# Audio-tower kernel on Trainium2: overflow rows of the tree feed-forward in groups of 128 with one leaf, tiles in pairs, levels added by halving

## What is computed

```
for _ in range(DEPTH + 1):                      # 8 levels
    all_nodes.append(current)
    score = jnp.einsum('td,td->t', flat_x, w1s[current]) + b1s[current]
    all_logits.append(score)
    choice = ((jnp.sign(score) + 1.0) / 2.0).astype(jnp.int32)
    current = current * 2 + choice + 1
path_weights = jax.nn.gelu(jnp.abs(logits), approximate=False)
for i in range(DEPTH + 1):
    t_i = jnp.einsum('td,tdo->to', flat_x, w2s[nodes_i]) + b2s[nodes_i]
    out = out + t_i * path_weights[:, i][:, None]
```

## Time and profile before

| what | value |
|---|---|
| device time, median of 3 runs | 558.85 us (558.7 to 559.1) |
| span of the profiled execution | 558.3 us |
| PE busy | 378.6 us (68%) |
| DVE busy | 369.1 us (66%) |
| ACT busy | 290.4 us (52%) |
| POOL busy | 273.7 us (49%) |
| DMA | 36.05 MB, mean 65 GB/s |

### The profile page before, as it was taken

One profiled execution on the slowest core, in us unless ns is written; L12 is line 12 of the kernel. 1 busy time (PEld: TensorE's weight loads), 2 busy tenths in 40 slices (PEclk: granted clock), 3 DMA queues, 4 the chain that ended last, 5 costly groups with the idle time before them and its releaser, 6 DMA issues.

```text
span 558.3 us, 8700 instructions
## 1 busy us (share of the span) xinstructions
PE 378.6 (68%) x3014; PEld 251.9 (45%) x3014; DVE 369.1 (66%) x596; ACT 290.4 (52%) x652; POOL 273.7 (49%) x316
## 2 busy tenths in 40 slices
PE   1212487888889978899588895475107997487781
PEld 1212353444547645476355652364105775254450
DVE  1295148777887779877878679625774999542431
ACT  1103466999986999869698695101101110144441
POOL 3036385333322468633658613838555777742211
PEclk9999997999999999999989998555557999599996
DMA  3500269839323332223303400380004110200000
GB/s 81 110 1 0 53 150 214 191 71 211 80 53 84 84 82 56 47 67 84 83 4 92 103 1 1 71 142 0 19 13 125 36 44 24 73 9 5 7 5 8
DMA packets 54530, 36.05 MB, mean 65 GB/s; under 512 B 25122, under 2 KB 53687, under 8 KB 54480
## 3 DMA queue, kind: packets, MB, share of 16 engines
q1 hardware_dynamic: 51538, 32.97, 27.7%
q0 software_dynamic: 2944, 2.45, 1.6%
HBM read 10.57 MB, written 8.79 MB: 35 GB/s over the span
## 4 chain that ended last, share of the span: by engine, by line
ACT 29%; PE 27%; DVE 25%; issue 8%; DMA 3%; SPq 3%; POOL 2%; POOLq 0%; DVEq 0%; ACTq 0%
ACT S L884 16%; PE S L697 6%; DVE nm L1031 5%; PE U L643 5%; DVE lm L1203 4%; ACT vT L871 4%; ACT k L871 3%; ACT q L871 3%; DVE vT L1196 3%; PE S L797 3%; PE U L604 2%; DMA vT<-in_L_attn_Wqkv 2%; PE U L797 2%; PE S L799 1%; SPq L282 1%
## 5 line engine op out<-in xcount | busy, mean ns | idle before, releaser
L1031 DVE TENSOR_REDUCE nm<-S 128x1 f32<-128x748 f32 x192 | 171.9, 932 | 44.3 <-PE S L697 41.7
L884 ACT ACTIVATE S<-S,nm 128x748 f32<-128x748 f32 x192 | 166.8, 883 | 42.4 <-DVE nm L1031 41.1
L697 PE MATMUL S<-pool_a 128*128 128x512 f16 (+1 forms) x768 | 151.4, 333 | 28.6 <-ACT S L884 26.0
L697 PEld LDWEIGHTS S<-pool_a 128*128 128x128 f16 x768 | 69.0, 105 | 91.4 <-ACT S L884 57.6
L520 POOL DMA_INDIRECT out<-lm,vT x44 | 43.3, 985 | 58.2 <-DVE lm L1209 51.2
L442 POOL TENSOR_TENSOR pool_a<-q,pool_a 128x750 f16<-128x750 f32 x16 | 25.8, 1610 | 82.4 <-DVE pool_a L1025 82.4
L604 PE MATMUL U<-xhT,wq 128*128 128x250 f16 x288 | 43.4, 292 | 21.0 <-ACT k L871 10.1
L1203 DVE TENSOR_REDUCE lm<-vT 128x64 f32<-128x512 f32 x44 | 45.1, 1026 | 1.3
L604 PEld LDWEIGHTS U<-xhT,wq 128*128 128x128 f16 x288 | 26.9, 104 | 39.6 <-ACT k L871 15.9
L884 ACT ACTIVATION_READ_ACCUMULATOR S<-S,nm 128x1 f32 x192 | 43.5, 226 | 0.0
L1196 DVE TENSOR_TENSOR vT<-vT 128x512 f32<-128x512 f32 x12 | 8.3, 693 | 41.9 <-ACT vT L953 41.9
(11 more groups left out here) (214 smaller groups left out, 666.8 us busy)
## 6 DMA issues: line engine op xcount, KB each, us to landing
pool_a<-pool_a SPq DMA_DIRECT2D x64, 187.5 KB, 3.0
pool_a<-pool_a SPq DMA_DIRECT2D x64, 93.8 KB, 2.8
sorted_rows<-zrow SPq DMA_DIRECT2D x1, 3864.0 KB, 22.6
vT<-sorted_rows SPq DMA_DIRECT2D x11, 276.0 KB, 3.7
w<-in_L_ffn_w2s SPq DMA_DIRECT2D x1, 2048.0 KB
lm<-in_x SPq DMA_DIRECT2D x4, 375.0 KB
pool_a<-in_L_ffn_w2s SPq DMA_DIRECT2D x1, 1024.0 KB
vT<-in_L_attn_Wqkv SPq DMA_DIRECT2D x2, 384.0 KB, 9.3
```

The source lines that it names most:

```text
L697: last = mm(S[n % 3][:, c0:c1], kst[:, u % 3, a, hd, START[t]:START[t] + P], qst[:, u % 3, hd, c0:c1], start=(a == 0), stop=(a == 1))
L884: sc_.activation(S[n % 3][:, 0:N], S[n % 3][:, 0:N], ACT.Exp, bias=nm[:, b % 2, j, i:i + 1], accum_out=sm[:, b % 2, j, i:i + 1]).then_inc( ...
L1031: v.tensor_reduce(nm[:, b % 2, j, i:i + 1], S[n % 3][:, 0:N], X, ALU.max, negate=True).then_inc(s_max, 1)
```

## The change

- **Groups.** An overflow group has 128 rows of one leaf and is a tile of its own. There is still space for 96 groups, which are now 96 tiles; `sorted_rows` grows from 7168 to 16384 rows, and SP fills it in four parts (w = 1 to 4), `w7` moves to w == 5. With the inputs given there are 29 groups, and 15 pairs of tiles run.
- **Products.** Levels 0 to 5 stand together in one table of 32 entries with six matrices each, so one product of 384 columns takes the place of those of 256 and 128; level 6 has a table `w6`. An overflow tile needs three products over all 128 rows; results lie where DVE wants them, so ACT's copies and `yv` go. Only the 65 rows in use are contracted, so POOL's zeros go.
- **Pairs.** Everything from `load_rows` to `add_residual` works on two tiles. A block `If` holds one pair instead of four tiles: 48 blocks, of which 15 run and 33 are skipped.
- **Sums.** The strided reduction becomes three halving additions (`levels_4`, `levels_2`, `levels_1`).
- **Order.** PE and ACT prepare pair m + 1 ahead of pair m, also across the border of the stages; SP loads the first overflow pair ahead of reading `nact`.
- **Space.** `xhT`, `wq`, `q32` and `k32` move into `pool_a`, which `wlow` and `w6` take over later.

```diff
...
-SLOTS = STAT + OVG * G
-ST_TILES, OV_TILES = STAT // P, OVG * G // P
+SLOTS = STAT + OVG * P
+ST_TILES, OV_TILES = STAT // P, OVG
 F_TILES = ST_TILES + OV_TILES
+FILLS = 4
...
-                if w == 1:
+                if 1 <= w <= FILLS:
 
                     sp.wait_ge(s_id, 2)
-                    sp.dma_start(rows.rearrange("(t p) c -> p t c", p=P),
-                                 zrow[:].unsqueeze(1).to_broadcast([P, F_TILES, RW])).then_inc(s_fill, 16)
...
+                    fl = slice((w - 1) * F_TILES // FILLS, w * F_TILES // FILLS)
+                    sp.dma_start(rows.rearrange("(t p) c -> p t c", p=P)[:, fl, :],
+                                 zrow[:].unsqueeze(1).to_broadcast([P, F_TILES // FILLS, RW])).then_inc(s_fill, 16)
+                if w == FILLS + 1:
...
             sp.wait_ge(s_score, 2 * NT * NU)
...
+            sp.wait_ge(s_prod, NU)
+            tv = wlow[:, 0:n_low].rearrange("p (n l o) -> p n l o", n=NODES5, l=6)
+            for rows_, src in ((slice(0, D), wv), (slice(D, D + 1), b2s.unsqueeze(0))):
+                for lv in range(6):
+                    n = 2 ** lv
+                    r = NODES5 // n
+                    m = D if src is wv else 1
+                    if n <= r:
+                        for i in range(n):
+                            sp.dma_start(tv[rows_, i * r:(i + 1) * r, lv, :],
+                                         src[:, n - 1 + i:n + i, :].to_broadcast([m, r, D])).then_inc(s_low, 16)
+                    else:
+                        for q in range(r):
+                            sp.dma_start(tv[rows_, q::r, lv, :], src[:, n - 1:2 * n - 1, :]).then_inc(s_low, 16)
+                sp.dma_start(w6[rows_, 0:2 * NODES5 * D].rearrange("p (n o) -> p n o", o=D),
+                             src[:, 2 * NODES5 - 1:4 * NODES5 - 1, :]).then_inc(s_low, 16)
...
+            def load_rows(m):
+                if m >= NX:
+
+                    for k in range(2 * (m - NX), 2 * (m - NX) + 2):
+                        sp.wait_ge(s_outr[k % NO], 16 * (k // NO + 1))
+                sp.dma_start(xs[:, m % NX], rv[:, 2 * m:2 * m + 2, :]).then_inc(s_xsr[m % NX], 16)
+
+            for m in range(ST_PAIRS):
+                load_rows(m)
             sp.wait_ge(s_goff, 1)
             sp.wait_ge(s_sego, 16 * TT)
+            load_rows(ST_PAIRS)
             groups = sp.value_load(nact[0:1, 0:1], min_val=0, max_val=OVG)
-            for k in range(ST_TILES // 4, F_TILES // 4):
-                with sp.If(groups > 4 * (4 * k - ST_TILES)):
-                    load_rows(k)
+            for m in range(ST_PAIRS, F_PAIRS - 1):
+                with sp.If(groups > 2 * (m - ST_PAIRS)):
+                    load_rows(m + 1)
...
-                       start=True, stop=True)
-                    mm(y[:, 7 * D:8 * D], xg, w7all[:, bass.ds(node(g, 0) * D, D)],
-                       start=True, stop=True).then_inc(s_y, 1)
-                return following
-
-            pe.wait_ge(s_goff, 1)
+            def overflow_pair(m):
+                leaves = [nc.tensor.value_load(lami[0:1, 2 * (m - ST_PAIRS) + t:2 * (m - ST_PAIRS) + t + 1],
+                                               min_val=0, max_val=LEAVES - 1) for t in range(2)]
+                pair_ready(m)
+                for t in range(2):
+                    y = y_banks(m)[:, 512 * t:512 * (t + 1)]
+                    xk = xsT[:, m % 3, t * P:(t + 1) * P]
...
+            for m in range(ST_PAIRS):
+                if m == 2:
+                    pe.wait_ge(s_goff, 1)
+                xs_T(m + 1)
+                static_pair(m)
             groups = pe.value_load(nact[0:1, 0:1], min_val=0, max_val=OVG)
-            for m in range(ST_TILES // 4, F_TILES // 4):
-                with pe.If(groups > 4 * (4 * m - ST_TILES)):
-                    xs_T(m)
-                    pairs = load_leaves(4 * m)
-                    for k in range(4 * m, 4 * m + 4):
-                        pairs = overflow_products(k, pairs)
+            for m in range(ST_PAIRS, F_PAIRS):
+                with pe.If(groups > 2 * (m - ST_PAIRS)):
+                    if m + 1 < F_PAIRS:
+                        xs_T(m + 1)
+                    overflow_pair(m)
...
-                    act.wait_ge(s_y, banks(4 * (m - 2)))
...
+                    act.wait_ge(s_y, m - 2)
+                sc_.copy(xsT[:, m % 3, :], S[0][0:D + 1, 512 * (m % 2):512 * (m % 2) + 2 * P]).then_inc(s_xc, 1)
+
+            for m in range(ST_PAIRS + 1):
                 path_weights(m)
                 xs_copy(m)
...
-            for m in range(ST_TILES // 4, F_TILES // 4):
-                with act.If(groups > 4 * (4 * m - ST_TILES)):
-                    path_weights(m)
-                    xs_copy(m)
-
-                    for k in range(4 * m, 4 * m + 4):
-                        if k >= ST_TILES + 2:
-                            act.wait_ge(s_wy, k - 1)
-                        for g in range(4):
-                            act.wait_ge(s_y, banks(k) + g + 1)
-                            sc_.copy(yv[g * G:(g + 1) * G, k % 2, :],
-                                     y_bank(banks(k) + g)[0:G, :]).then_inc(s_yv, 1)
+            for m in range(ST_PAIRS, F_PAIRS - 1):
+                with act.If(groups > 2 * (m - ST_PAIRS)):
+                    path_weights(m + 1)
+                    xs_copy(m + 1)
...
-            def weigh(k):
...
+            def weigh(m):
...
+                wk = xs[:, m % NX, :, C_W:C_H]
+                v.tensor_tensor(wy[:, m % 2], y_banks(m)[:].rearrange("p (t l o) -> p t l o", t=2, l=DEPTH),
+                                wk.unsqueeze(3).to_broadcast([P, 2, DEPTH, D]), ALU.mult).then_inc(s_wy, 1)
+
+            def levels_4(m):
+                dve.wait_ge(s_wy, m + 1)
+                w = wy[:, m % 2]
+                v.tensor_tensor(w[:, :, 0:4, :], w[:, :, 0:4, :], w[:, :, 4:8, :], ALU.add).then_inc(s_s1, 1)
+
+            def levels_2(m):
+                dve.wait_ge(s_s1, m + 1)
+                w = wy[:, m % 2]
+                v.tensor_tensor(w[:, :, 0:2, :], w[:, :, 0:2, :], w[:, :, 2:4, :], ALU.add).then_inc(s_s2, 1)
+
+            def yo_pair(m):
+                return yo[:, 2 * m % NO:2 * m % NO + 2, :]
+
+            def levels_1(m):
+                for k in range(2 * m, 2 * m + 2):
+                    if k >= NO:
+                        dve.wait_ge(s_outr[k % NO], 16 * (k // NO))
+                dve.wait_ge(s_s2, m + 1)
+                w = wy[:, m % 2]
+                v.tensor_tensor(yo_pair(m), w[:, :, 0, :], w[:, :, 1, :], ALU.add).then_inc(s_sl, 1)
+
+            def add_residual(m):
+                dve.wait_ge(s_sl, m + 1)
+                o = yo_pair(m)
+                v.tensor_tensor(o, o, xs[:, m % NX, :, C_H:C_ID], ALU.add).then_inc(s_yo, 1)
+
+            for m in range(ST_PAIRS):
+                weigh(m)
+                if m >= 1:
+                    levels_1(m - 1)
+                levels_4(m)
+                if m >= 1:
+                    add_residual(m - 1)
+                levels_2(m)
+            levels_1(ST_PAIRS - 1)
+            add_residual(ST_PAIRS - 1)
             dve.wait_ge(s_goff, 1)
             groups = dve.value_load(nact[0:1, 0:1], min_val=0, max_val=OVG)
-            for m in range(ST_TILES // 4, F_TILES // 4):
-                with dve.If(groups > 4 * (4 * m - ST_TILES)):
-                    for k in range(4 * m, 4 * m + 4):
-                        weigh(k)
-                        sum_levels(k)
-                        add_residual(k)
+            for m in range(ST_PAIRS, F_PAIRS):
+                with dve.If(groups > 2 * (m - ST_PAIRS)):
+                    weigh(m)
+                    levels_4(m)
+                    levels_2(m)
+                    levels_1(m)
+                    add_residual(m)
...
```

229 lines of the change are left out of this document (72 added, 157 removed).

## The result

The changed kernel takes **587.56 us** (median of four runs, 587.39 to 588.28), the kernel before 558.98 beside it (558.7 to 559.36): a ratio of 1.0511, 95% interval 1.0496 to 1.0526. The forecast was 556.5 us, its range 549 to 566. It was wrong by 31 us and in the sign. The profiled execution took 587.61 us, its span is 585.9.

The account below looks back on a forecast made before the run. DVE and POOL nearly fill the static stage; overflow is a chain of waits. Overflow's 58.5 us become 49.2; of 9.3 won, 3.7 go to later start, 1.3 to the second output, 2 to the end: 556.5 us, range 549 to 566.

Parts of the forecast that it names:

- The first pair: Start of the static stage: DVE needs two tiles before weighing, so the first output comes 4.3 us later, at 434.3.
- The static stage: Static tiles cost nothing more: DVE 2.94 us a pair, PE about 3.1, both hidden behind POOL's 5.1.
- The overflow stage: Overflow tiles: DVE bounds at 3.28 us a pair, PE 3.0 to 3.5; 15 pairs take 49.2 us, last residual at 543.0.
- list of what costs nothing: Fill, table loads, POOL's zeros and DVE's packing, mostly ahead of the static stage: costed at nothing; 1 to 3 us if units wait.
- Nothing before 415 us changes in a way that I can cost at more than its cover: Everything ahead of the static stage: no change there counted, so the sum covers only about the last 143 us.
- The border: Static to overflow: PE idles some 12 us for overflow rows, restarts at the lower clock; first overflow weighing at 493.8.
- The end: After the last output at 545.1: 33 skipped blocks on every engine, SP, POOL and PE ending near 555, span 556.
- rival 2: End of the kernel: POOL's closing drain is a fixed 8 us behind its skips, giving 559.9 us; chance 0.18.
- rival 1: End of the kernel: PE's way through the skipped blocks takes 28.2 us and ends last, giving 563.5 us; chance 0.14.
- Rival 3: Overflow tiles: PE bounds at 3.6 us a pair if register loads stop it and its clock falls, 561 us; chance 0.12.
- The fill: Filling sorted_rows ahead of the static stage: grows from 3.9 to 9 MB, costed at nothing, 1 to 3 us if units wait.

Follow-up runs that it names:

- fourth set: Changed kernel with 128 rows contracted in the 384-column products only, their table's zeros written by ScalarE, empty overflow pairs skipped eight at once: 553.32 us, 0.9898 of the kernel before.
- the blocks: POOL and SP skip empty overflow pairs eight at once, against the changed kernel with 128 rows and its zeros moved (582.90 us): 579.19 us, 0.9855 of the kernel before.

## Why the prediction was wrong

The step that failed is in "The first pair" and "The static stage": the clock of the earlier trace rows, 0.93, was carried over to products whose operands had changed from 128 rows to 65. The same holds for PE's price in "The overflow stage", 1024 columns at 1.8 ns: 3.0 to 3.5 us a pair by it, 4.58 measured at 0.50, so that PE bounds the pair and not DVE. In the forecast's list of what costs nothing, the zeros appear only as "POOL's zeros end 33 us before they could matter". That the rows they fill take part in every product, and what a product of fewer rows does to the clock, was not asked. Point by point:

- **The first pair**: first output 4.3 us later, at 434.3. Measured 430.28. From the transposes to it, it is 14.2 us against 7.7, so 6.5 later by itself, 2.2 more than forecast. The forecast had the upper level from the second tile on, as before, where it came 4.2 us behind the first transpose. That was wrong apart from the 65 rows: with 128 rows on the fourth set's chip it came 9.5 us behind it, and the first output after 13.6 us. But the stage starts at 416.1, 6.3 us earlier. "Nothing before 415 us changes in a way that I can cost at more than its cover" was wrong.
- **The static stage** costs nothing more: right in its result, wrong in its reason. POOL went on without a gap up to 477.16 (forecast 479.3), in 46.9 us for the 45.0 forecast, as some scatters took up to 1.5 us and not 0.98; PE at 5.05 us a pair instead of 3.1 is just as fast as POOL's 5.1 to 5.2, by chance.
- **The border**: 12 us idle, restart at the lower clock, first overflow weighing at 493.8. In the changed kernel PE never idles there, it is late itself, and that weighing is at 502.7. With 128 rows (fourth set) PE idles 12.46 us and the weighing comes at 492.3.
- **The overflow**: DVE 3.28 us a pair, PE 3.0 to 3.5. Measured: PE 4.58, DVE waiting 1.4 us in each pair. Fourteen pitches of 1.30 us more make 18.2 us (67.4 us from the first weighing to the last residual at 570.1, 49.2 forecast), the largest term of the miss. With the clock up, DVE took 3.07 and PE less (it waited for DVE's banks); the stage took 46.3 us against 49.2 forecast.
- **The end**: SP 9.8 us behind the last output, measured 9.3; POOL's skips 5.6 us, measured 5.4, of which 1.0 lie ahead of the last output's start; its closing step lasts 9.06 us from its own start, behind the skips (8.0 before), and does not end 8.6 us after the last output. That is rival 2, and it came: 13.7 us of tail, not 10. PE's walk past the empty blocks took 15.9 us (561.3 to 577.2), 20 forecast, 28.2 under rival 1, which fell: 5 waits of 0.6 to 2.0 us in it, none of 3.9.
- **Rival 3** (PE bounds the overflow if "its clock falls again") had the right engine and the wrong cause and size: 3.6 us a pair for a fall after idling, where PE never idled and needed 4.58.
- **The fill** (1 to 3 us lost at most): it lost nothing, and its four pieces are half of what won 5.5 us.

In sum: the overflow starts 8.9 us later than forecast (502.7 for 493.8), takes 18.2 more, from its last residual to the end of the span it is 15.8 us and not 13.0, and the runs stand 1.7 us above the span, not 0.5: 8.9 + 18.2 + 2.8 + 1.2 = 31.1, which is what was missed. The Trainium skill (TensorE: Matmul & The Clock Gate, "What's actually happening") ties the upper level to how busy the engine has been. The trace does not agree as far as busy is read as it is in the profile: PE was busy 56.00 of 56.00 us and at 0.50. Why fewer rows keep the clock down no run here shows; that they do is shown both ways.

## What to carry to other kernels

Zero rows that a product multiplies are not idle weight: before you drop them, look up the granted clock of the stage and ask whether it would survive, and keep them under the largest products at least; here that is worth some 31.5 us of the changed kernel's 588, and 35 together with the blocks. The rows of an operand are part of the price of a product, not at a given clock (1.49 us both ways) but by the clock they leave, so a duration taken from a row with `128*128` isn't a row for `65*128`. And a memset or a large fill that is put "where it doesn't matter" has three customers: its own engine's queue, the neighbour whose steps it holds (VectorE's, here, for up to 5.25 us), and the DMA queue behind it. Moving it only changes which step it meets.
